# A convolution and local attention kernel: values of an image three steps later, V in three parts, both masks ahead of the scores

## What is computed

```python
perceived = depthwise_conv3x3(x, w_perc) + b_perc          # 3 filters a channel: 384 channels
hid = gelu(w_up1 @ perceived + b_up1)                      # 256
h   = x + w_up2 @ hid + b_up2                              # 128
q, k, v = split(w_qkv @ h + b_qkv)
w   = softmax(q . k over the 3 x 3 neighbours / sqrt(128)) # zero keys outside the image
out = h + sum(w * v over the 3 x 3 neighbours)
```

## Time and profile before

| what | value |
|---|---|
| median of 3 runs | 434.16 us (433.71 to 434.34) |
| the profiled execution | 436.07 us |
| its span, first to last instruction | 434.2 us |
| PE busy | 406.6 us (94%) |
| PE weight loads busy | 345.8 us (80%) |
| DVE busy | 350.0 us (81%) |
| ACT busy | 272.2 us (63%) |
| POOL busy | 177.1 us (41%) |
| mean granted clock of TensorE | 0.995 |
| HBM traffic | 20.51 MB read, 8.39 MB written |

### The profile page before, as it was taken

How to read it: one execution, slowest core, us unless ns; L and a number is a source line. 1 busy time by engine, 2 the same in 40 slices (tenths; PEclk the granted TensorE clock), 3 DMA queues, 4 the chain that set the end, 5 groups by cost and what they waited for, 6 DMA issues and landing times.

```text
span 434.2 us, 9715 instructions
## 1 busy us (share of the span) xinstructions
PE 406.6 (94%) x3572; PEld 345.8 (80%) x3572; DVE 350.0 (81%) x656; ACT 272.2 (63%) x643; POOL 177.1 (41%) x155
## 2 busy tenths in 40 slices
PE   1397998999999999999999999999999999999895
PEld 1397696988979798888979798897979888897774
DVE  5997569797897979798897979889797979865666
ACT  5414177748565866747576774756586674856683
POOL 6577065243634524353453414363452435310100
PEclk9999899999999999999999999999999999999999
DMA  8210301031130403122040403113040311110003
GB/s 275 104 48 18 112 4 48 2 114 51 57 107 2 161 2 116 45 92 69 10 151 0 155 6 112 48 53 108 0 161 0 117 44 50 51 48 2 2 2 145
DMA packets 11366, 29.20 MB, mean 67 GB/s; under 512 B 2384, under 2 KB 3024, under 8 KB 11344
## 3 DMA queue, kind: packets, MB, share of 16 engines
q1 hardware_dynamic: 10640, 28.89, 19.4%
q10 hardware_dynamic: 704, 0.02, 0.1%
HBM read 20.51 MB, written 8.39 MB: 67 GB/s over the span
## 4 chain that ended last, share of the span: by engine, by line
PE 84%; DVE 10%; ACT 2%; issue 2%; ACTq 0%; POOL 0%; DVEq 0%
PE m_ps L414 43%; PE work L429 12%; PE work L469 8%; PE work L435 6%; PE work L440 6%; PE s_ps L453 6%; PE s_ps L449 2%; DVE wlo L752 1%; DVE t L746 1%; DVE y L821 1%; DVE y L824 1%; DVE s_ps L770 1%; DVE ptc L875 1%; ACT hid L589 1%; DVE y L826 1%
## 5 line engine op out<-in xcount | busy, mean ns | idle before, releaser
L414 PE MATMUL m_ps<-thi,whi 128*128 128x256 f32 x576 | 180.6, 313 | 5.7 <-POOL wlo L1038 4.8
L414 PE MATMUL m_ps<-thi,wlo 128*128 128x256 f32 x576 | 162.4, 282 | 0.0
L414 PE MATMUL m_ps<-tlo,whi 128*128 128x256 f32 x576 | 162.3, 282 | 0.0
L414 PEld LDWEIGHTS m_ps<-thi,whi 128*128 128x128 f32 x576 | 109.4, 190 | 15.7 <-issue 12.2
L414 PEld LDWEIGHTS m_ps<-tlo,whi 128*128 128x128 f32 x576 | 109.4, 190 | 7.2 <-issue 7.2
L414 PEld LDWEIGHTS m_ps<-thi,wlo 128*128 128x128 f32 x576 | 109.2, 190 | 0.0
L1029 POOL TENSOR_TENSOR p_sb<-p_sb,rsum 128x384 f32<-128x384 f32 x32 | 27.8, 870 | 153.2 <-DVE rsum L864 153.2
L589 ACT ACTIVATE hid<-y,b1eff 128x1024 f32<-128x1024 f32 x31 | 35.7, 1152 | 85.2 <-DVE y L834 61.5
L1022 POOL TENSOR_TENSOR tlo<-t,thi 128x1088 fp32r<-128x1088 f32 (+1 forms) x32 | 63.5, 2011 | 57.0 <-ACT thi L573 57.0
L628 ACT COPY pt<-ptc 32x256 f32<-32x256 f32 (+3 forms) x189 | 74.0, 392 | 6.0 <-DVE ptc L875 1.4
L429 PE MATMUL work<-hid,w2T 128*128 128x512 f32 x120 | 55.8, 609 | 3.6 <-ACT hid L589 3.6
(11 more groups left out here) (109 smaller groups left out, 599.8 us busy)
## 6 DMA issues: line engine op xcount, KB each, us to landing
xp<-x_planes SPq DMA_DIRECT2D x16, 680.0 KB, 4.6
xr<-x_rows SPq DMA_DIRECT2D x16, 512.0 KB, 3.4
out<-o_sb SPq DMA_DIRECT2D x28, 256.0 KB, 2.1
out<-y SPq DMA_DIRECT2D x4, 256.0 KB, 2.1
w1T<-w SPq DMA_DIRECT2D x1, 384.0 KB, 3.0
w2T<-w SPq DMA_DIRECT2D x1, 128.0 KB, 4.7
wqk_in<-w_qk SPq DMA_DIRECT2D x1, 128.0 KB, 4.5
mask_bf<-masks SPq DMA_DIRECT2D x1, 120.0 KB, 3.7
```

What stands on the lines that cost most here:

```text
L414: last = pe.matmul(m_ps[:, b, col:col + S], a[:, j, dy, half * P:(half + 1) * P], c[:, par, T_PLACE[j], dy * WIN:dy * WIN + S], start=(s = ...
```

## The change

It does the following:

- V comes in three parts of 3, 3 and 2 tiles in place of four of 2. Part 3's matmuls, between units 7 and 8, go into the others. The zero keys of the scores still come in four operations (`Z_PARTS`).
- Values in step n are those of image n-3, and both groups stand right before up, after units 0 to 3. They go to the two banks of `s_ps`, which the scores of the step before have left. `add_h` stands on DVE between `transform` and `sum_h`, and `sum_h` waits for it (h of image n-3 is overwritten). Stores follow by one step.
- In steps 1 to 15 both masks are written first and then both groups of scores; each mask waits for the exps of the step before and for `add_h` of its bank.
- In `last_attention` the scores stay apart. V part 1 now has three tiles and stands behind the wait for the second h_done, V part 2 two. The values of the last three images have other banks.

```diff
-        V_PARTS = (range(0, 2), range(2, 4), range(4, 6), range(6, 8))
+        V_PARTS = (range(0, 3), range(3, 6), range(6, 8))
+        Z_PARTS = (((0, 0, 3), (1, 0, 1)), ((1, 1, 3), (2, 0, 2)))
...
-            if isinstance(n, int) and n > B:
-                return m_ps[:, g, :]
-            return work[:, (2, 0)[g], :]
+            if isinstance(n, int) and n >= B:
+                return ((work[:, 2, :], work[:, 0, :]), (m_ps[:, 1, :], m_ps[:, 2, :]),
+                        (work[:, 1, :], m_ps[:, 0, :]))[n - B][g]
+            return s_ps[:, g, :]
...
-            def scores(n, hp, g):
-                if from_image(n, 2):
-
-                    pe.wait_ge(p_done, n * 8 + (4 * g - 12))
+            def scores(n, hp):
+                for g in range(2):
+                    if from_image(n, 2):
+
+                        pe.wait_ge(p_done, n * 8 + (4 * g - 12))
+                    if from_image(n, 3) and not is_last(n):
+
+                        pe.wait_ge(o_done, n * 2 + (g - 5))
+                    mask_scores(g)
+                for g in range(2):
+                    score(n, hp, g)
...
                 pe.wait_ge(y_done, n * 2 + 1)
                 project_v(n, hp, 0)
+                pe.wait_ge(h_done, n * 2)
                 project_v(n, hp, 1)
-                pe.wait_ge(h_done, n * 2)
                 pe.wait_ge(q_done, n * 2 - 1)
...
+                if attn and from_image(n, 3):
+                    for g in range(2):
+                        values(n, 1 - par, g)
                 if attn:
                     up(n, 0)
                     up(n, 1)
...
-                    scores(n, 1 - par, 0)
-                    scores(n, 1 - par, 1)
-                units(7)
-                if attn:
-                    pe.wait_ge(z_done, n * 4 - 3)
-                    project_v(n, 1 - par, 3)
-                units(8, 9)
-                if store and not before_last(n):
-                    values(n, par, 0)
-                units(10)
-                if store and not before_last(n):
-                    values(n, par, 1)
-                units(11)
+                    scores(n, 1 - par)
+                units(7, 8, 9, 10, 11)
...
             def sum_h(n, par):

+                if from_image(n, 3) and not is_last(n):
+
+                    dve.wait_ge(o_done, n * 2 - 4)
...
                 if more:
                     transform(n + 1, 1 - par)
+                if attn and from_image(n, 3):
+                    for g in range(2):
+                        add_h(n, 1 - par, g)
                 if from_image(n, 2) and attn:
                     sum_h(n, par)
```

More of the change, by code:

```diff
@@ L293, in v_bank @@
             if is_last(n):
-                return (m_ps[:, 2, :], work[:, 1, :], m_ps[:, 0, :], m_ps[:, 1, :])[part]
-            return work[:, (1, 2, 0, 1)[part], :]
+                return (m_ps[:, 2, :], work[:, 1, :], m_ps[:, 0, :])[part]
+            return work[:, (1, 2, 0)[part], :]
         def o_bank(n, g):
-            if is_last(n):
-                return (m_ps[:, 2, :], work[:, 1, :])[g]
-            if isinstance(n, int) and n > B:
-                return m_ps[:, g, :]
-            return work[:, (2, 0)[g], :]
+            if isinstance(n, int) and n >= B:
+                return ((work[:, 2, :], work[:, 0, :]), (m_ps[:, 1, :], m_ps[:, 2, :]),
+                        (work[:, 1, :], m_ps[:, 0, :]))[n - B][g]
+            return s_ps[:, g, :]
         def s_bank(g):
@@ L343, in store_out @@
                 for g in range(2):
-                    sp.wait_ge(o_done, n * 2 - 3 + g)
-                    sp.dma_start(out[n - 2][:, g * CH:(g + 1) * CH],
+                    sp.wait_ge(o_done, n * 2 - 5 + g)
+                    sp.dma_start(out[n - 3][:, g * CH:(g + 1) * CH],
                                  o_sb[:, g * CH:(g + 1) * CH]).then_inc(stored[g], 16)
@@ L365, in body @@
                     load_rows(n + 1, 1 - par)
-                if store and not before_last(n):
+                if store and from_image(n, 3):
                     store_out(n)
@@ L442, in project_v, with mask_scores, score @@
                 last.then_inc(v_ready, 1)
-            def scores(n, hp, g):
-                if from_image(n, 2):
-                    pe.wait_ge(p_done, n * 8 + (4 * g - 12))
+            def scores(n, hp):
[7 more added lines that the diff above has]
+                    score(n, hp, g)
+            def mask_scores(g):
+                pe.matmul(s_bank(g)[:, :, 0:NEAR], ident_bf[:, :], mask_bf[:, g:g + 4, :], start=True, stop=False,
+                          skip_group_check=True)
+            def score(n, hp, g):
                 s = s_bank(g)[:, :, 0:NEAR]
-                pe.matmul(s, ident_bf[:, :], mask_bf[:, g:g + 4, :], start=True, stop=False, skip_group_check=True)
                 for u in range(4):
@@ L452, in scores @@
                         q = ((4 * g + u) * TR + row) * W
-                        last = pe.matmul(s[row * W:(row + 1) * W, u, :], q_sb[:, q:q + W], h_of(n - 1, hp)[:, q:q + NEAR],
-                                         start=False, stop=(u == 3 and row == TR - 1), skip_group_check=True)
+                        last = pe.matmul(s[row * W:(row + 1) * W, u, :], q_sb[:, q:q + W],
+                                         h_of(n - 1, hp)[:, q:q + NEAR], start=False, stop=(u == 3 and row == TR - 1),
+                                         skip_group_check=True)
                 last.then_inc(s_ready, 1)
             def values(n, hp, g):
[L459 to L463, removed]
+                if not isinstance(n, int) or n < B:
+                    pe.wait_ge(v_done, n * 3 - 6)
+                    pe.wait_ge(pt_done, n * PLACED - 2 * PLACED)
+                    pe.wait_ge(p_done, n * 8 + (4 * g - 12))
                 half = T // 2 * TR
@@ L468, in values @@
                     above = i * TR - 1
-                    last = pe.matmul(o_bank(n, g)[:, (first - g * half) * W:(end - g * half) * W], v_of(n - 2, hp)[:, i, :],
+                    last = pe.matmul(o_bank(n, g)[:, (first - g * half) * W:(end - g * half) * W], v_of(n - 3, hp)[:, i, :],
                                      pt[:, hp, i, (first - above) * W:(end - above) * W], start=(i == blocks[0][0]),
@@ L491, in last_attention @@
                 project_v(n, hp, 0)
+                pe.wait_ge(h_done, n * 2)
                 project_v(n, hp, 1)
-                pe.wait_ge(h_done, n * 2)
                 pe.wait_ge(q_done, n * 2 - 1)
-                scores(n, hp, 0)
+                pe.wait_ge(p_done, n * 8 - 12)
+                pe.wait_ge(o_done, n * 2 - 7)
+                mask_scores(0)
+                score(n, hp, 0)
                 project_q(n, hp, 1, 0)
                 project_v(n, hp, 2)
-                project_v(n, hp, 3)
                 pe.wait_ge(q_done, n * 2)
-                scores(n, hp, 1)
+                pe.wait_ge(p_done, n * 8 - 8)
+                pe.wait_ge(o_done, n * 2 - 6)
+                mask_scores(1)
+                score(n, hp, 1)
                 pe.wait_ge(pt_done, (n - 2) * PLACED)
                 for g in range(2):
-                    values(n - 1, 1, g)
-                pe.wait_ge(v_done, n * 4 - 2)
+                    values(n, 1, g)
                 pe.wait_ge(z_done, n * 4 - 2)
@@ L508, in last_attention @@
                 for g in range(2):
-                    values(n, 0, g)
-                pe.wait_ge(v_done, n * 4)
+                    values(n + 1, 0, g)
+                pe.wait_ge(v_done, n * 3)
                 pe.wait_ge(z_done, n * 4)
@@ L514, in last_attention @@
                     pe.wait_ge(pt_dve_done, 9 + 6 * g)
-                    values(n + 1, 1, g)
+                    values(n + 2, 1, g)
             def body(n, par, conv, attn, store, more):
@@ L840, in take_v @@
                 sums = v_bank(n, part)[:, 0:len(tiles) * VT].rearrange("p (t c) -> p t c", c=VT)
-                dve.wait_ge(v_ready, n * 4 + (part - 3))
+                dve.wait_ge(v_ready, n * 3 + (part - 2))
                 nc.vector.tensor_tensor(v_of(n - 1, hp)[:, first:end, :], sums[:, :, 0:C],
@@ L849, in row_max @@
                 dve.wait_ge(s_ready, n * 2 + (g - 1))
[L850 to L854, removed]
+                for part, first, end in Z_PARTS[g]:
+                    tiles = V_PARTS[part][first:end]
+                    z = v_bank(n, part)[:, 0:len(V_PARTS[part]) * VT].rearrange("p (t c) -> p t c", c=VT)[:, first:end, C:VT]
+                    dve.wait_ge(v_ready, n * 3 + (part - 2))
+                    nc.vector.tensor_tensor(s[:, tiles[0] - 4 * g:tiles[-1] + 1 - 4 * g, NEAR:KEYS],
+                                            z.to_broadcast([P, len(tiles), NZ]), z_base[:, tiles[0]:tiles[-1] + 1, :],
                                             ALU.add).then_inc(z_done, 1)
@@ L879, in add_h @@
                 cols = slice(g * CH, (g + 1) * CH)
[L880 to L884, removed]
+                dve.wait_ge(o_ready, n * 2 + (g - 5))
```

(16 more changed lines are left out.)

5 lines of the change are left out of this document (removed).

## The result

The changed kernel takes 430.97 us (median of 7 runs, 430.86 to 433.19) against 434.34 us for the kernel before in the same comparison; the ratio is 0.9907, 95% interval 0.9882 to 0.9932. The forecast was 431.2 in a range of 428.8 to 433.6.

A forecast was written before the change was run, and what follows sets the result against it. PE's own work was taken to bound the steady step. Boundaries 0, masks -3.3 and the last image +0.3 gave -3.0 us from the median 434.16, so 431.2 us, in a range of 428.8 to 433.6.

The forecast's parts named there:

- PE alone bounds the step: Middle step, up to up: PE busy for 24.78 of 24.78 us, so only work removed from PE's sequence gains.
- Boundaries cost nothing: Passages between fp32 and fp32r matmuls on PE: joining V and values groups removes 0 to 0.03 us a step.
- Rival 2: Boundaries do cost: 0.08 us each, three a step over 15 steps, 3.6 us more gained, 427.6 us; chance 0.06.
- Masks together: First mask to fp32r work on PE, steps 1 to 15: 0.22 us a step saved, 3.3 us in all.
- the run of 16 fours: Both groups of scores in one run on PE, four tiles side by side: 0.62 + 0.09 + 0.62 = 1.33 us.
- Rival 1: Half a saving: only the seam from scores to mask goes, 0.09 to 0.14 us a step, 432.8 us; chance 0.14.
- the exit: Passage on PE from the last scores to the unit behind them: 0.90 - 0.62 = 0.28 us.
- The last image: Three-tile V part 1 puts 12 records, not 8, before the first mask: 0.34 us lost, from 0 to 0.44.
- h_done: DVE's signal before V part 0 comes at U + 4.6 (U: start of up), slack 1.0 us, no PE wait.
- the U + 4.7: Sign of being right: second sum_h ended by 4.7 us after the start of up, lasting 0.75 us despite low_t.
- Rival 3: POOL's low_t holds up sum_h, h_done at U + 6.5, PE waits 0.9 us in steps 3 to 14, 442 us; chance 0.09.
- Rival 4: Eaten up: small new PE waits, 0.2 us a step, at unit 9 and m13 or later h_done, 434.2 us; chance 0.09.

The follow-up runs named there:

- experiment 5: Changed kernel plus one 512-column DVE operation (0.6 us) between the two add_h and sum_h, steps 3 to 15: median 432.32 us, ratio 0.9936.
- experiment 2: Changed kernel with each mask again directly ahead of its own scores; V in three parts and values ahead of up stay: 434.88 us, ratio 0.9994.
- experiment 1: Kernel before with only the masks moved, both ahead of both groups of scores in steps 1 to 15: 431.35 us, ratio 0.9913.
- experiment 3: Two kernels, each the kernel before with values moved: both groups joined between units 9 and 10, ratio 0.9992; in four pieces between units, ratio 0.9989.
- experiment 6: Kernel before with both masks ahead of the scores in steps 1 to 15, and the last image's second q ahead of masks and scores: 430.50 us.
- experiment 4: Changed kernel with both masks ahead of V part 1, not directly ahead of the scores: median 432.11 us, ratio 0.9941.

## Why the prediction was right, point by point

- **PE alone bounds the step.** Right: 24.55 us of 24.55 busy, and the added DVE operation of experiment 5 costs something only where it holds up PE.
- **Boundaries cost nothing.** Right: 0 to 0.03 us a step was forecast, experiment 2 gives 0.04 for V and values together (0.01 to 0.02 beside experiment 1), and experiment 3 0.00 for one boundary fewer and 0.02 less for two more. Rival 2 (427.6) falls.
- **Masks together, 0.22 us a step.** Right in place, a little small: 0.24. The forecast's own pieces add up to 2.03 us, which saves only 0.19; the 0.22 was put above its sum. The weakest piece was the run of 16 fours (four scores side by side), taken as 1.33 us from a mean gap of 0.09: its starts spread over 1.28 us, since the gap between fours is 0.083 and only the first is longer, 0.106. With the exit, 0.28 as forecast, that is 1.56 us where 1.61 was forecast; the masks and their seam are 0.42, as forecast. Rival 1 (half a saving) falls: mask to mask is 0.16. The rule of the Trainium skill ("TensorE: Matmul & The Clock Gate", The mechanism), that a weight load overlaps matmuls in flight only when its row group differs, does not describe this trace either; the same section also lets a load into the background weight buffer go ahead, and with that the hidden load of the second mask agrees.
- **The last image, +0.34.** Right: measured +0.36, and experiments 1 and 2 put it on V's parts: 25.30 with four, 25.64 with three.
- **h_done.** The outcome, no wait, was right partly by luck, since the working was off: I gave U + 4.6 and a slack of 1.0 us. It came at U + 5.14 to U + 5.20 in steps 5 to 13, past the U + 4.7 that was to show the forecast right. The slack was 0.2 us by experiment 5, because I also set h_done against V part 0's matmul and not against its weight load. DVE, ACT and POOL of the changed kernel around the up at 216.43:

```profile
207.72 0.69 DVE L816 TENSOR_TENSOR ps_sb<-m,m_ps 128x512 f32<-128x512 f32 x1 [0.48 <-ACT m L585]
...
216.19 0.69 DVE L816 TENSOR_TENSOR ps_sb<-m,m_ps 128x512 f32<-128x512 f32 x1 [1.17 <-ACT m L585]
...
220.22 1.41 DVE L949 SCALAR_TENSOR_TENSOR h_around<-work,b,xr 128x512 f32<-128x512 f32 x2
221.55 1.45 DVE L826 TENSOR_TENSOR y<-ps_sb 128x256 f32<-128x256 f32 x1
```

```profile
206.91 0.60 ACT L585 COPY m<-m_ps 128x512 f32<-128x512 f32 x1
...
214.35 1.15 ACT L595 ACTIVATE hid<-y,b1eff 128x1024 f32<-128x1024 f32 x1 [4.01 <-DVE y L840]
```

```profile
220.18 4.01 POOL L1030 TENSOR_TENSOR tlo<-t,thi 128x1088 fp32r<-128x1088 f32 x2 [3.60 <-ACT thi L579]
```

  The second combine (207.72) waits for ACT's copy of m13, where I let the two meet at unit 9's end; m13 is ready 5.5 us behind the first mask, not 5.4, and unit 9 is early. With that the gelu ends at U - 0.9 and not U - 1.2 (with the masks apart, in experiment 2, the second `sum_h` ends at U + 4.93, so the masks' new place accounts for most of this). A second mistake: I let an operation start when its input's record ends, and both combines start 0.2 us behind the end of the copy. So the first combine starts at U - 0.2 and not U - 0.7. The rest is `sum_h`'s wait for `add_h`, 0.2 us between starts, which I had put under the wait for up; DVE comes later than up, so both stand in line.
- **Rival 3, POOL holding up sum_h.** It falls: the second `sum_h` lies wholly within `low_t` (220.18 on) and takes 0.74 us, as before; the pair takes 1.41. The next operation, with two inputs in SBUF, is again held up (1.45 us, where the one at U - 7.0, begun while POOL is idle, takes 0.39). This is as the Trainium skill has it ("SBUF — State Buffer", Who interferes with whom): a VectorE instruction with at most one SBUF input does not contend with GpSimd.
- **Rival 4, small new waits.** None in the changed kernel, but it was nearer than its chance of 0.09 says: 0.2 us more on DVE would have begun to bring it.
- **The sum.** Forecast from the median 434.16 it was -3.0 us; measured between 434.34 and 430.97 it is -3.4. The rest is 0.02 to 0.03 us a step in 15 steps.

## What to carry to other kernels

Before joining groups of matmuls, compare the distance between the starts before and behind one group with what its matmuls take at their own rate; if the two agree, the boundary is free, however long the first record behind it looks. Look instead for a change of the array's shape: at the seams between masks and scores the passage from full-width matmuls to those with 32 output partitions cost about 0.1 us here and the way back as much, so put all narrow work of a step into one run and the wide work around it outside. Where a step is moved, its chain behind other engines' copies must be laid out again to a tenth of a microsecond: the change kept its gain with 0.2 us to spare, not with the 1.0 that a rough layout gave. Measure the spare time up to the weight load where the weights are what is waited for.

## What the runs showed of the hardware that I had not expected

The same kernel's executions differ by about 1.7 us through one event. In some, the granted clock falls to 1.2 GHz within the first up, after PE has been idle for 2.0 to 2.1 us ahead of it (2.3 between the starts); in others, with the same wait, it stays at 2.4 GHz. Of the profiles here, the kernel before, the changed one, the masks apart, and experiments 5 and 6 have it (step 1 of 25.2 to 25.5 us), the masks alone, the values joined, in four pieces and the masks ahead of V don't (23.5 to 23.7). With the wait filled by 18 matmuls no run of the 11 of the two kernels lay in the upper group, while 3 of the 11 runs of the kernel before beside them did, and so did 1 of the 7 runs of the changed kernel, 2 of the 6 of the masks alone and 4 of the 8 of experiment 4. That PE's idle time has a part in it is what the filling shows, as far as 11 runs can; what decides between the runs of one kernel stays open.
